# A fused attention and feed-forward block in float32 split in two parts: roundings, first maxima, biases and the tail in another order

## The reference

```python
def attn(xq, ctx, wq, wkv, wo, bo):
    q = rope(heads(xq @ wq)); k, v = split(ctx @ wkv); k = rope(heads(k)); v = heads(v)
    a = softmax(q @ k.T * 64 ** -0.5)
    return merge(a @ v) @ wo + bo
def adaln(x, c, lw, lb, gw, gb, bw, bb):
    return layernorm(x, lw, lb) * (1 + c @ gw + gb) + (c @ bw + bb)
h = adaln(x, cond, ...ln1...);  x = attn(h, h, sa_...) + x
h = adaln(x, cond, ...ln1...);  x = attn(h, layernorm(context), ca_...) + x
h = adaln(x, cond, ...ln2...);  x = gelu(h @ w1 + b1) @ w2 + b2 + x
```

## Time and profile before

| | us |
|---|---|
| median of 3 runs | 1116.58 |
| lowest and highest | 1114.38 and 1116.66 |
| the profiled execution | 1118.88 |
| its span, first to last instruction | 1117.1 |

### The profile page before, as it was taken

One profiled execution on the slowest core, in us unless ns is written; L12 is line 12 of the kernel. 1 busy time (PEld: TensorE's weight loads), 2 busy tenths in 40 slices (PEclk: granted clock), 3 DMA queues, 4 the chain that ended last, 5 costly groups with the idle time before them and its releaser, 6 DMA issues.

```text
span 1117.1 us, 18312 instructions
## 1 busy us (share of the span) xinstructions
PE 1097.2 (98%) x6904; PEld 785.1 (70%) x6904; DVE 858.1 (77%) x1023; ACT 636.9 (57%) x895; POOL 775.7 (69%) x503
## 2 busy tenths in 40 slices
PE   8989999999999999999999999999999999989998
PEld 7657666776666776666766667766666776756997
DVE  5878887878787777878888777777877777788554
ACT  6465565665666555577665555555555545775521
POOL 2687887787788767789799766777777667755210
PEclk9899999999999999999999999999999999999999
DMA  6312121311231111211121112211121111300001
GB/s 175 86 46 57 32 53 39 89 30 30 53 77 38 39 36 23 72 39 39 29 63 38 39 39 59 51 23 36 38 72 39 37 31 30 114 1 1 20 19 38
DMA packets 59606, 52.31 MB, mean 47 GB/s; under 512 B 23040, under 2 KB 42496, under 8 KB 59264
## 3 DMA queue, kind: packets, MB, share of 16 engines
q1 hardware_dynamic: 57632, 49.57, 18.5%
q10 hardware_dynamic: 1888, 1.59, 0.5%
HBM read 15.22 MB, written 2.10 MB: 16 GB/s over the span
## 4 chain that ended last, share of the span: by engine, by line
PE 90%; DVE 5%; ACT 2%; issue 1%; DMA 1%; SPq 0%; POOL 0%; ACTq 0%; POOLq 0%; DVEq 0%
PE ps L872 18%; PE ps L713 12%; PE ps L715 11%; PE ps L714 11%; PE ps L813 6%; PE ps L860 6%; PE ps L848 5%; PE ps L819 5%; PE ps L815 5%; PE ps L817 5%; PE ps L963 4%; DVE lo L1083 1%; PE ps L729 1%; DMA x<-x_dram 1%; DVE w_lo L1117 1%
## 5 line engine op out<-in xcount | busy, mean ns | idle before, releaser
L548 ACT ACTIVATE probs<-ps 128x1024 f32<-128x1024 f32 x256 | 262.5, 1027 | 208.0 <-PE ps L819 183.6
L1065 DVE TENSOR_REDUCE neg_max<-ps 128x2 f32<-128x1024 f32 x256 | 301.6, 1226 | 76.7 <-PE ps L848 76.7
L420 POOL TENSOR_TENSOR acc<-acc,probs 128x1024 f32<-128x1024 f32 x128 | 306.2, 2392 | 18.6 <-POOL acc L415 0.4
L872 PE MATMUL ps<-probs,v 128*64 128x512 f32 x1024 | 230.7, 592 | 0.0
L415 POOL TENSOR_TENSOR acc<-probs 128x1024 f32<-128x1024 f32 x64 | 153.2, 2394 | 72.1 <-ACT probs L548 72.1
L872 PEld LDWEIGHTS ps<-probs,v 128*64 128x64 f32 x1024 | 73.9, 137 | 146.1 <-issue 146.1
L429 POOL TENSOR_TENSOR eo<-tmp 128x512 f32<-128x512 f32 x63 | 89.7, 1424 | 120.2 <-DVE tmp L1092 120.1
L1092 DVE TENSOR_TENSOR tmp<-ps,rope 128x1024 f32<-128x1024 f32 x126 | 148.2, 1211 | 4.5 <-PE ps L715 4.3
L813 PE MATMUL ps<-max_rows,pick 64*128 64x512 f32 x512 | 109.3, 419 | 2.6 <-DVE o_lo L1079 1.6
L713 PE MATMUL ps<-xn_hi,w_hi 128*128 128x512 f32 x256 | 107.8, 421 | 2.5 <-DVE o_lo L1079 1.3
L848 PE MATMUL ps<-hi 64*128 64x512 f32 x512 | 104.8, 400 | 5.4 <-DVE neg_max L1065 2.6
(11 more groups left out here) (116 smaller groups left out, 2250.0 us busy)
## 6 DMA issues: line engine op xcount, KB each, us to landing
...
max_rows<-neg_max SPq DMA_DIRECT2D x128, 2.0 KB, 2.0
...
```

Of the source, the lines that this page charges most:

```text
L420: pool.tensor_tensor(acc[:, g % 2, :, :], acc[:, g % 2, :, :], probs[:, i, :, :], ALU.add).then_inc(added, 1)
L548: act.activation(probs[:, i, :, :], score_ps(i), ACT.Exp, scale=SCALE).then_inc(exped, 1)
L872: mm = pe.matmul(av_ps[DH * h:DH * h + DH, :], v[:, u % 2, kt, c:c + DH], probs[:, kt, h, :], start=(kt == 0), stop=(kt == TT - 1))
L1065: dve.tensor_reduce(neg_max[:, g % 2, :, i], peak_ps(i), AX.X, ALU.max, negate=True).then_inc(maxed, 1)
```

## The change

Eight edits, all of order or of what is waited for:

1. ScalarE does `high_qk(p+2)` right behind the exponentials, ahead of `guess_inverse(p-1)` and of a normalisation's rows.
2. VectorE does `low_qk(p+2)` right behind the maxima, ahead of `normalise(p-1)`. The low part of pair 1 goes to GpSimd, behind its rotation of job 3, with a semaphore of its own.
3. SyncE sends the maxima of pair 0 (`land_max(0)`) ahead of job 2's landing.
4. TensorE projects job 3 in four pieces between and behind the peaks of pair 0, ahead of the transposes of norm 2.
5. The self attention's biases go from periods 0, 1, 5, 7 to 13, 15, 18, 21; `add_out` waits for a bias only from quad 8 on, and the bias waits for the addition of the batch's second quad.
6. In period 61 VectorE does statistics ahead of `normalise`; the average of pair 61 goes to bank 5, and the waits of the scores of pair 62 on `av_kept` and `o_low` go to the first maxima of pair 63.
7. The feed-forward weights' low parts are made in one instruction of 128x2048 for each matrix in place of four.
8. GpSimd adds only two of the last pair's four probability tiles; VectorE adds the other two into `tmp`, and TensorE sums both with twice the matmuls.

Before, the four peaks had only the modulation between them, and all twelve matmuls of job 3 stood behind the transposes. The diff's core:

```diff
@@ -126,7 +126,9 @@
         def sum_ps(g):
             return ps[:, {PAIRS - 1: 6, PAIRS - 4: 4}.get(g, 0), :]
 
-        av_ps = ps[:, 1, :]
+        def av_ps(g):
+            return ps[:, 5 if g == PAIRS - 3 else 1, :]
+
         ada_ps = (ps[:, 0, :], ps[:, 1, :])
         side_ps = (ps[:, 5, :], ps[:, 6, :])
...
@@ -234,7 +238,7 @@
         turned_in = {at[2]: n for n, at in norm_at.items()}
         low_in = {at[2] + 1: n for n, at in norm_at.items() if at[2]}
         bias_in = {at[0] + 3: n for n, at in norm_at.items() if n >= NB and at[1] is not None and order[n][0] == X}
-        bias_in.update({0: 0, 1: 1, 5: 2, 7: 3})
+        bias_in.update({13: 0, 15: 1, 18: 2, 21: 3})
 
         bias_in.pop(PAIRS - 2)
...
@@ -363,8 +367,8 @@
             load_x(2)
             land(0)
             land(1)
+            land_max(0)
             land(2)
-            land_max(0)
             load_x(3)
             load_ctx(0)
...
@@ -434,6 +438,8 @@
                 sublayer = sum(1 for kind, _, _ in order[:n] if kind == X) // NB
                 pool.wait_ge(rows_in, 16)
                 pool.wait_ge(ln_rows, TT * (n + 1))
+                if sublayer == 0:
+                    pool.wait_ge(o_added, 2 * (NB + b) + 2)
                 pool.tensor_tensor(x[:, b, :, :], x[:, b, :, :],
                                    bias_rows[:, sublayer, :].unsqueeze(1).broadcast_to([128, TT, D]),
...
@@ -444,8 +450,9 @@
                     norm_split(pool, low_in[p], 1)
                 if is_pair(p):
                     add_probs(p, 1)
-                    add_probs(p, 2)
-                    add_probs(p, 3)
+                    if p < PAIRS - 1:
+                        add_probs(p, 2)
+                        add_probs(p, 3)
                 if p in stats_in:
                     refine_rstd(pool, stats_in[p])
...
@@ -467,6 +474,8 @@
             norm_split(pool, 2, 0)
             norm_split(pool, 2, 1)
             rotate(3)
+            pool.wait_ge(qk_high, 2)
+            pool.tensor_tensor(lo[:, 1, :, :], raw_qk[:, 1, :, :], hi[:, 1, :, :], ALU.subtract).then_inc(qk_low_1, 1)
             for p in range(PAIRS):
                 period(p)
...
@@ -596,12 +605,12 @@
                 if is_pair(p):
                     for i in range(TT):
                         exp(p, i)
+                if is_pair(p + 2):
+                    high_qk(p + 2)
                 if is_pair(p - 1):
                     guess_inverse(p - 1)
                 if p in rows_in_period:
                     norm_rows(rows_in_period[p])
-                if is_pair(p + 2):
-                    high_qk(p + 2)
                 if p in split_in:
                     split_weights(*split_in[p])
...
-                    if j == 3 and e == 1:
-                        pe.wait_ge(maxed, 3)
+                    if j == 1:
+                        pe.wait_ge(roped, e + 1)
                     for kt in range(KT):
                         c = slice(kt * 256 + e * 128, kt * 256 + (e + 1) * 128)
                         mm = parts(job_ps(j, e), w_hi[0:rows, k, c], w_lo[0:rows, k, c],
                                    a_hi[0:rows, b, kt, :], a_lo[0:rows, b, kt, :], kt == 0, kt == KT - 1)
+                    mm.then_inc(projected, 1)
+
+
+            def project_3(e, kt):
+                if e == 0 and kt == 0:
+                    pe.wait_ge(w_split, 2)
+                    pe.wait_ge(ln_split, 4)
+                if e == 1 and kt == 0:
+                    pe.wait_ge(maxed, 3)
+                c = slice(kt * 256 + e * 128, kt * 256 + (e + 1) * 128)
+                mm = parts(job_ps(3, e), w_hi[:, 0, c], w_lo[:, 0, c], xn_hi[:, 1, kt, :], xn_lo[:, 1, kt, :],
+                           kt == 0, kt == 1)
+                if kt == 1:
                     mm.then_inc(projected, 1)
 
...
@@ -794,11 +814,14 @@
                     pe.wait_ge(ln_scaled, 5)
                     pe.wait_ge(roped, 7)
                 if kt == 0:
-                    pe.wait_ge(qk_low, g + 1)
+                    if g == 1:
+                        pe.wait_ge(qk_low_1, 1)
+                    else:
+                        pe.wait_ge(qk_low, max(g, 1))
                     pe.wait_ge(max_landed, 32 * (g + 1))
-                    if g > 0:
+                    if g > 0 and g != PAIRS - 2:
                         pe.wait_ge(av_kept, g)
-                    if g > 1:
+                    if g > 1 and g != PAIRS - 2:
                         pe.wait_ge(o_low, g - 1)
                 if kt == 1 and g - 1 in turned_in:
...
@@ -835,6 +858,7 @@
                     side_free(p - 1, i)
                     if i == 0 and p == PAIRS - 2:
                         pe.wait_ge(o_low, PAIRS - 3)
+                        pe.wait_ge(av_kept, PAIRS - 2)
                     if g == 1 and i == 1:
...
@@ -849,15 +873,19 @@
                 mm.then_inc(peaked, 1)
 
             def total(g):
-                pe.wait_ge(added, 3 * g + 3)
+                pe.wait_ge(added, 3 * g + (3 if g < PAIRS - 1 else 1))
                 if g == PAIRS - 4:
                     pe.wait_ge(maxed, 4 * (g + 2) + 3)
                 elif is_pair(g + 1):
                     pe.wait_ge(exped, 4 * (g + 1) + 3)
                 else:
                     pe.wait_ge(o_added, 2 * (QUADS - 1))
+                    pe.wait_ge(last_added, 1)
                 for h in range(2):
-                    mm = pe.matmul(sum_ps(g)[DH * h:DH * h + DH, :], ones[:, :], acc[:, g % 2, h, :], start=True, stop=True)
+                    out = sum_ps(g)[DH * h:DH * h + DH, :]
+                    mm = pe.matmul(out, ones[:, :], acc[:, g % 2, h, :], start=True, stop=g < PAIRS - 1)
+                    if g == PAIRS - 1:
+                        mm = pe.matmul(out, ones[:, :], tmp[:, 0, h, :], start=False, stop=True)
                 mm.then_inc(summed, 1)
 
...
@@ -923,11 +951,14 @@
             peak(0, 0)
             peak(0, 1)
             modulate(3)
+            project_3(0, 0)
             peak(0, 2)
+            project_3(0, 1)
             peak(0, 3)
+            project_3(1, 0)
+            project_3(1, 1)
             norm(2, 0)
             norm(2, 1)
-            project(3)
             for p in range(PAIRS):
                 period(p)
...
@@ -1101,7 +1132,7 @@
 
             def add_out(u, r):
                 _, b, phase = quad(u)
-                if r == 0:
+                if r == 0 and u >= 2 * NB:
                     dve.wait_ge(biased, NB * phase + b + 1)
                 dve.wait_ge(o_projected, 2 * u + r + 1)
                 rows = x[:, b, 2 * r:2 * r + 2, :]
@@ -1109,47 +1140,44 @@
                 dve.tensor_tensor(rows, out.rearrange("p (t d) -> p t d", d=D), rows, ALU.add)\
                    .then_inc(o_added, 1)
 
-            def split_ffw(m, c):
-                cut = slice(c * N, (c + 1) * N)
-                dve.wait_ge(ffw_high, 4 * m + c + 1)
+            def split_ffw(m):
+                dve.wait_ge(ffw_high, 4 * m + 4)
                 high, low, raw = ((w1_hi, w1_lo, w1_raw), (w2_hi, w2_lo, w2_raw))[m]
-                flat = [t.rearrange("p k f -> p (k f)") for t in (high, low, raw)]
-                dve.tensor_tensor(flat[1][:, cut], flat[2][:, cut], flat[0][:, cut], ALU.subtract)\
-                   .then_inc(ffw_split, 1)
+                dve.tensor_tensor(low[:, :, :], raw[:, :, :], high[:, :, :], ALU.subtract).then_inc(ffw_split, 1)
+
+            def add_last_probs():
+                dve.wait_ge(exped, 4 * PAIRS)
+                dve.tensor_tensor(tmp[:, 0, :, :], probs[:, 2, :, :], probs[:, 3, :, :], ALU.add).then_inc(last_added, 1)
 
             def period(p):
                 u = p // 2
                 if is_pair(p + 1):
                     for i in range(TT):
                         peak(p + 1, i)
-                if p == 0:
-                    low_qk(1)
+                if is_pair(p + 2):
+                    low_qk(p + 2)
+                if p == PAIRS - 3:
+                    norm_stats(stats_in[p])
                 if is_pair(p - 1):
                     normalise(p - 1)
-                if p in stats_in and p != PAIRS - 3:
-                    norm_stats(stats_in[p])
+                if p == PAIRS - 1:
+                    add_last_probs()
+                if p in stats_in:
+                    if p != PAIRS - 3:
+                        norm_stats(stats_in[p])
                     norm_means(stats_in[p])
                 if is_pair(p - 1):
                     low_o(p - 1)
-                if p == PAIRS - 3:
-                    norm_stats(stats_in[p])
-                    norm_means(stats_in[p])
                 if p == PAIRS - 2:
-                    for c in range(4):
-                        split_ffw(0, c)
-                if is_pair(p + 2) and p not in stats_in:
-                    low_qk(p + 2)
+                    split_ffw(0)
                 if is_job(p + 4):
                     rotate(p + 4, 0)
                     rotate(p + 4, 1)
-                if is_pair(p + 2) and p in stats_in:
```

(4 more changed lines are left out.)

14 lines of the change are left out of this document (7 added, 7 removed).

## The result

The changed kernel takes 1151.46 us (1149.49 to 1153.51), the kernel before in the same rounds 1115.48 (1114.35 to 1116.66): a ratio of 1.0323, interval 1.0298 to 1.0347. The forecast was 1140, with a range of 1110 to 1156 and 0.74 on slower. The sign, the mechanism and the range held; of +36 us the sum had +23. The profiled execution took 1150.72 us, its span is 1148.9, 31.8 longer than before.

What follows compares the result with a forecast made beforehand. TensorE, busy for 98% of the span, was taken as the bound. Terms +21 + 9 - 2.5 - 6.3 + 0.7 + 1.5 = +23.4 us on the profiled 1118.88 gave 1142.3, or 1140 for the median; range 1110 to 1156.

Steps and rivals of the forecast that it cites:

- Part 1, plain periods: Middle, even periods: low_qk waits for GpSimd's addition, normalise is late, project_out waits for o_low; 20 x 1.05 = 21 us lost.
- Slack of 1.37 us: Plain even period: o_low ends at 942.81, project_out starts at 944.18; a delay within this costs nothing.
- Part 1, the landing: Periods behind statistics and transposed ones: high_qk's late landing holds guess_inverse, rotations come late; 9 us lost, bounds 2 and 16.
- the nine: Periods 6, 10, 14, 18, 28, 30, 32, 34 and 60, taken together; forecast +13.2 us.
- rival (c): Much slower: TensorE's repeated stalls bring it to 1.2 GHz in half of 24 periods; +18, 1158 us; chance 0.12.
- Part 2, the biases: Biases leave periods 0, 1, 5 and 7, so waits for late additions to x end; 2.5 us gained, bound 0 to 2.5.
- Part 3, the start: Start: project(3) fills TensorE's gaps, scores of pair 0 come 2.9 us earlier; 6.3 us gained, 0.7 lost in period 2.
- Part 4, the tail: Tail: the stall for o_low moves to peak(63,0) and grows, +1.4 by project_out(30); net +1.5 us, bounds -4 and +4.
- (a): Faster: low_qk gets in ahead of GpSimd's second addition, the slack covers the delay; -6.6 us, 1110; chance 0.20.
- (b): No change: about a third of the stalls come, 7 to 9 us, cancelled by the ends; chance 0.06.

Runs made afterwards that it cites:

- e4: The changed kernel, with GpSimd's second addition of the probabilities in a period made to wait until VectorE's low_qk is done: 1129.86 us, ratio 1.0128.
- e11: The changed kernel, with GpSimd's second addition of the probabilities split into two instructions of half the columns each: 1123.49 us, ratio 1.0066.
- e10: The changed kernel with edit 5 alone undone, biases again in periods 0, 1, 5 and 7: 1148.32 us, ratio 1.0288.
- e3: The changed kernel with high_qk and low_qk both back in their old places, keeping start, biases, tail and last sum: 1111.43 us, ratio 0.9965.
- e7: The changed kernel with the old order of ScalarE and VectorE in periods 6, 10, 14, 18, 28, 30, 32, 34, 60 alone: 1132.61 us, ratio 1.0143.

## Why the prediction was right, and where it was off

**Part 1, plain periods: right.** Slack of 1.37 us, low_qk behind the running addition, normalise 2.2 us late (2.16 measured), a stop per even period. The step's price was 1.05 and measured 0.86. The trace's idle time ahead of project_out is 0.57 to 0.65; it is counted from the end of the last matmul, while matmuls of 0.39 us normally start 0.22 us apart, so each stop moves project_out by 0.17 more (12.97 for 12.14 in period 58). The forecast's 0.1 for a refill behind the stop did not come on top (15.91 for 15.07). The count was twenty with 6, 10, 14 and 18; sixteen are plain. e4 and e11 show the cause, not only the place. The 3.0 us too many here hide a part of the 9.5 too few in the next term.

**Part 1, the landing: right in kind, too small by 9.5 us in the nine.** The failing step is the sentence that 28, 30, 32, 34 and 60 "run a normalisation's transposes (0.8 us) ahead of project_out and lose only about 0.1 each". It looked at o_low as the only thing that project_out's side waits for. The transposes wait for rows on ScalarE, and the rows stand behind high_qk and its landing, which the held low_qk makes later still: 2.1 to 4.3 us in each of the five, 14.7 in all, where the forecast had 3.2. Three half-clock stretches of about 1.6 us, in 14, 28 and 34, are a part of rival (c), which had 12 in 100; it came in 3 periods, all behind stops of 1.9 to 2.24 us, in none of the plain ones with stops of 0.57 to 0.65, and once more in the tail.

**Part 2, the biases: the number right, the reason wrong.** -2.3 for -2.5 in the odd periods, but e10 shows them there with the biases at the old place. So the step of the forecast that ties the 2.5 us to the biases failed. By the medians the changed kernel is 3 us slower than e10 (1151.46 and 1148.32, from different rounds). Of this the traces show 2.3, and the half clock in 14 and 28, which e10 has in neither, makes more than that; whether the moved biases cost anything by themselves is not shown.

**Part 3, the start: nearly right, in this trace.** -5.2 for -6.3. Scores of pair 0 started at 39.99, 3.2 us earlier (2.9 forecast); periods 0 and 1 gave 1.9 of the 3.4 expected, and in e3, without low_qk in front, 2.9. The size depends on where the half clock falls: e7 has the same instructions in these periods, full clock from 25 to 50 us (0.93 in the changed kernel's trace) and a lower one behind it, and its gain is 3.8 in place of 5.2.

```profile
25.00:50.00 25.00, 21.72 (x127) 15.42 (x126) 20.28 (x34) 15.29 (x23) 14.78 (x15) 1.00 0.46 121
50.00:75.00 25.00, 22.34 (x131) 16.56 (x131) 18.44 (x24) 14.23 (x23) 20.46 (x16) 0.93 0.11 22
```

So this term moves by 1.4 us between executions of the same instructions, and 5.2 is the larger of the two.

**Part 4, the tail: the sum right, by two errors that cancel.** +1.8 for +1.5. The stall moved on to the first maxima of pair 63, as forecast: o_low ends 14.19 us behind the start of period 61, before 11.09, so 3.1 later for the forecast's 3.3. But the stop is 3.48 us long and half clock follows it:

```profile
1022.54 0.81 PE L872 MATMUL ps<-hi 64*128 64x512 f32 x2 [3.48 <-DVE o_lo L1110]
...
1023.00:1028.00 5.00, 5.00 (x26) 4.20 (x26) 2.80 (x3) 2.25 (x3) 2.70 (x6) 0.50 0.02 3
```

project_out(30) comes 3.8 us later against the start of period 61 (26.80 for 23.03), not 1.4. Behind it 2.0 us come back: the stop at the second hidden block is 0.29 us in place of 1.27 and no half clock follows it now, where the granted clock before was 0.65 in 1018.19 to 1023.

e3 shows what stands behind this: with both orders back the same tail is 3.3 us shorter than before (135.6 us from the start of period 61 to the end, before 138.9), so the tail's edits gain and the two orders lose 5 there.

**The rivals.** (a), the gain of 6.6 us with low_qk ahead of the second addition, is what e4 forces in the plain periods (15.07 us); the nine (+15.6) keep even that from being a gain. (b), stalls that the ends cancel, did not come.
